# Layer 1's attention of one batch and layer 0's of the next, run as one attention of seven units

## What is computed

```python
for layer in (0, 1):
    h = layernorm(x) * (1 + ca) + sa
    x = x + ga * attention(h)        # 16 heads of 8, causal, 1024 tokens
    h = layernorm(x) * (1 + cb) + sb
    x = x + gb * experts(h)          # layer 0: 8 experts, best 2; layer 1: 16 experts, gated, best 4
# attention of layer 0: softmax(h K^T) V for all heads, then gelu, Wf, bias, residual h
# attention of layer 1: rotary q and k; 6 plain heads, 4 hyperbolic heads, 6 cosine heads
def hyp_attn(q, k, v, curv):
    inner = q k^T - sqrt(1/curv + |q|^2) * sqrt(1/curv + |k|^2)
    arg = maximum(-curv * inner, 1 + 1e-7)
    scores = 1 / (1e-6 + sqrt(1/curv) * arccosh(arg)) + causal
    return softmax(scores) v
```

## Time and profile before

| what | us |
|---|---|
| median of 3 runs (lowest, highest) | 2570.61 (2569.86, 2571.68) |
| the profiled execution | 2583.2 |
| its span, first to last instruction | 2580.8 |
| start, to the first score product of block 0 | 80.2 |
| attention of layer 0, batches 0 to 3 | 159.0, 159.8, 163.0, 161.3 |
| from there to the first score product of layer 1 (gelu, projection, layer norm, ffn(0), `prepare`), batch 1 | 118.4 |
| attention of layer 1, batches 0 to 3 | 214.7, 212.0, 211.8, 206.4 |
| output projection of layer 1, batch 1 | 8.1 |
| layer norm and ffn(1) of batch 1, with the guests of batch 2 | 127.7 |
| the same for batch 3, without guests | 112.1 |

### The profile page before, as it was taken

How to read it: one execution, slowest core, us unless ns; L and a number is a source line. 1 busy time by engine, 2 the same in 40 slices (tenths; PEclk the granted TensorE clock), 3 DMA queues, 4 the chain that set the end, 5 groups by cost and what they waited for, 6 DMA issues and landing times. The chain is left out here.

```text
span 2580.8 us, 29914 instructions
## 1 busy us (share of the span) xinstructions
PE 2141.7 (83%) x10649; PEld 851.2 (33%) x10649; DVE 1481.4 (57%) x3042; ACT 1345.0 (52%) x1923; POOL 832.4 (32%) x909
## 2 busy tenths in 40 slices
PE   6798967779999886678999987777899998677889
PEld 2232422224433342223443333222443324322243
DVE  6562557756556266675655435777665634577552
ACT  2345447973244545795224543688423454378922
POOL 1112124543411313552331221355232211145534
PEclk7899857778999896677999987667899998676789
DMA  5200231004310023100620012110051002301012
GB/s 147 66 14 12 72 99 35 2 1 123 97 28 1 18 80 85 36 1 13 157 59 20 2 50 83 48 36 1 27 153 41 20 2 83 89 10 36 1 53 87
DMA packets 67845, 128.31 MB, mean 50 GB/s; under 512 B 11396, under 2 KB 24836, under 8 KB 63076
## 3 DMA queue, kind: packets, MB, share of 16 engines
q1 hardware_dynamic: 67696, 126.40, 17.8%
HBM read 109.99 MB, written 15.20 MB: 49 GB/s over the span
## 5 line engine op out<-in xcount | busy, mean ns | idle before, releaser
L1267 DVE TENSOR_REDUCE mx<-ps 128x1 f32<-128x512 f32 (+3 forms) x992 | 612.5, 655 | 377.8 <-PE ps L607 246.9
L1015 ACT ACTIVATE pr<-ps 128x1024 f32<-128x1024 f32 (+3 forms) x672 | 515.8, 805 | 407.6 <-PE ps L677 407.0
L604 PE MATMUL ps<-kop,qop 72*128 72x512 bf16 (+6 forms) x1248 | 430.1, 378 | 110.3 <-DVE mx L1267 68.7
L677 PE MATMUL ps<-qop,kop 75*128 75x512 bf16 (+7 forms) x1344 | 412.1, 370 | 118.0 <-DVE wb L1329 41.6
L1558 POOL TENSOR_SCALAR_AFFINE_SELECT pr<-pr 128x512 f32<-128x512 f32 x224 | 144.9, 647 | 739.8 <-ACT pr L1015 739.1
L723 PE MATMUL ps<-pr,vt 128*32 128x512 f32 (+3 forms) x2688 | 339.5, 582 | 8.4 <-POOL pr L1558 7.8
L1076 ACT ACTIVATE pr<-ps 128x512 f32<-128x512 f32 x224 | 133.8, 598 | 341.9 <-PE ps L832 278.3
L604 PEld LDWEIGHTS ps<-kop,qop 72*128 72x128 bf16 (+1 forms) x1248 | 129.4, 106 | 443.5 <-DVE mx L1267 256.8
L677 PEld LDWEIGHTS ps<-qop,kop 75*128 75x128 bf16 (+1 forms) x1344 | 121.9, 105 | 357.1 <-ACT pr L1015 116.7
L842 PE MATMUL ps<-pr,w_down 128*128 128x512 f32 x384 | 196.5, 598 | 4.1 <-POOL pr L1549 4.1
L829 PE MATMUL ps<-hT,w_gate 128*128 128x512 f32 x384 | 196.2, 592 | 0.2 <-DVE on L1494 0.2
(11 more groups left out here) (313 smaller groups left out, 3089.1 us busy)
## 6 DMA issues: line engine op xcount, KB each, us to landing
wb<-gates_scratch SPq DMA_DIRECT2D x192, 256.0 KB, 3.4
kop<-kparts_scratch SPq DMA_DIRECT2D x32, 576.0 KB
qop<-qparts_scratch SPq DMA_DIRECT2D x96, 192.0 KB
on<-hmax_scratch SPq DMA_DIRECT2D x8, 1024.0 KB, 5.6
kparts_scratch<-on SPq DMA_DIRECT2D x12, 256.0 KB, 2.9
qparts_scratch<-on SPq DMA_DIRECT2D x12, 256.0 KB, 4.5
qparts_scratch<-wb SPq DMA_DIRECT2D x12, 192.0 KB
kparts_scratch<-wb SPq DMA_DIRECT2D x12, 192.0 KB
```

Source lines behind the costliest of these rows:

```text
L604: mm = pe.matmul(o, qop[0:k, slot(l, u), j, qb * P:(qb + 1) * P], kop[0:k, slot(l, u), j, k0:k0 + wd], start=True, stop=not diag)
L677: mm = pe.matmul(o, kop[0:k, slot(l, u), 2 * pair + j, kb * P:(kb + 1) * P], qop[0:k, slot(l, u), 2 * pair + j, q0:q0 + wd], start=True, s ...
L1015: nc.scalar.activation(pr[:, g % 3, 2 * pair:2 * pair + 2, o0:o0 + wd], ps[:, bank:bank + 2, o0:o0 + wd], ACT.Exp).then_inc(a.exps, 1)
L1267: ins_ = nc.vector.tensor_reduce(mx[:, nth(l, u) % 2, j0:j0 + heads, qb, col % 2], ps[:, bank, 0:heads * wd].rearrange("p (j n) -> p j n", ...
```

## The change

Block b now holds the attention of layer 1 of batch b-1 and that of layer 0 of batch b as one loop over seven units, 84 positions, in the order of `units`. The experts of layer 1 come one block later (batch b-2), and there are six blocks. Block 4 has layer 1's attention of batch 3 alone, with half-steps at positions 2 to 25; block 5 the last ffn(1).

```diff
-HYP_POS = [1 + k for k in range(HYP_HALVES)]
+def units(b):
+    if b == 0:
+        return [(0, 0), (0, 1), (0, 2), (0, 3)]
+    if b < B:
+        return [(1, 0), (0, 0), (0, 1), (1, 1), (0, 2), (0, 3), (1, 2)]
+    return [(1, 0), (1, 1), (1, 2)] if b == B else []
+def hyp_positions(b):
+    if 1 <= b < B:
+        return [3 + 3 * k if k < 8 else 32 + 3 * (k - 8) for k in range(HYP_HALVES)]
+    return [2 + k for k in range(HYP_HALVES)] if b == B else []
...
+    elif b < B:
+        hyp_pieces(0, 0, 1)
+        unit_pieces(1, 2, 8)
+        unit_pieces(2, 15, 20)
+        hyp_pieces(1, 24, 28)
+        unit_pieces(3, 28, 32)
+        for n in (4, 5, 6):
+            unit_pieces(n, NS * (n - 1) + 3, NS * (n - 1) + 8)
+        for c in range(NC):
+            plan[36 + c].append(("xT", (c,)))
```

Standard units now alternate between two of the three operand slots, the hyperbolic unit keeps the third, and each unit's operands are loaded when the unit two before it has ended. The hyperbolic values no longer accumulate in PSUM, since bank 5 holds layer 0's sums: a side job "hv" multiplies one step (two half-steps) into bank 6 or 7, and VectorE adds it to `hacc`:

```diff
+                    elif kind == "hv":
+                        i = what[0]
+                        c, kb, q0, wd, _ = STEPS[i]
+                        o0 = q0 - c * CH
+                        acc, o = hacc[:, o0:o0 + wd], ps[:, bank, o0:o0 + wd]
+                        if kb == 0:
+                            ins_ = nc.vector.tensor_copy(acc, o)
+                        else:
+                            dve.wait_ge(J.side_out, count("hv", (i - 1,)))
+                            ins_ = nc.vector.tensor_tensor(acc, o, acc, ALU.add)
```

More of the change, by code:

```diff
@@ L15 @@
 SLOTS = 3
-HYP_RING = 5
 PAIRS = 3 * HD * 3
@@ L53, with layer @@
 OPS_HYP = OPS + 16 * (1 + 2)
+HYP = 7
+def units(b):
[4 more added lines that the diff above has]
+    return [(1, 0), (1, 1), (1, 2)] if b == B else []
+UN = [units(b) for b in range(B + 2)]
+def layer(b, n):
+    return 1 if n == HYP else UN[b][n][0]
 def diagonals(g):
```

1295 lines of the change are left out of this document (666 added, 629 removed).

## The result

| what | before | after |
|---|---|---|
| median (lowest to highest) | 2570.91 (2569.86 to 2571.68) | 2810.62 (2807.57 to 2832.83) |
| the profiled execution | 2583.2 | 2832.8 |
| its span | 2580.8 | 2831.1 |
| its two attentions of a pair, or its joint attention, three of each | 374.5, 375.0, 373.1 | 456.9, 453.7, 454.9 |

The changed kernel takes 1.0951 times as long (95% interval 1.0895 to 1.1008). 2652 us were forecast; the measured median lies outside the range of 2495 to 2720 us. All rows of the changed kernel come from its one profiled execution, which was 0.8% (22 us) over its median. The window of the first joint attention starts 0.8 us ahead of its first score product, the others at theirs.

A forecast was written before the change was run, and what follows sets the result against it. Layer 0's attention was taken as TensorE's, layer 1's as ScalarE's. Other terms summed to +4.4 us, so span = 1462.6 + 3 J; J = 400 gave 2662.6, execution 2665.0, scaled to the median 2652 us, range 2495 to 2720.

The forecast's parts named there:

- J: Time of one joint attention of seven units, forecast at 400 us; the kernel gets slower if it is over 372.7 us.
- Start: First maxima's DMA waits behind late loads until 80.2 us; with 3 MB less in front, -4.5 us (0 to -7).
- Block 1's operands and the barrier: Batch 1's operands run alone, uncovered by ffn(1), +30 us (22 to 36); one more barrier, +1.5 us.
- The stretches before blocks 2, 3 and 4: Between attentions: ffn(1) -1, -1 and -15.6 us, output of layer 1 half hidden, -4 us each.
- eleven first hyperbolic groups: Batch 3's attention: formerly run during a load wait, now after the border with nothing to hide them, +7 us (0 to 10).
- Reloading 4 MB of weights in a block: DMA is little busy and no load is waited for: 0 us; without that cover 18 us a block.
- I ask of every position which engine has most in it: Joint attention priced position by position by its largest engine, since engines go in step; gave J = 400 us.
- windows with pieces: Joint attention: five wide positions with 7.2 groups each, VectorE largest at 6.8 us a position, 34 us together.
- The plain positions: Positions without pieces, one half-step in three: 14.3 us for three wide ones, against 8.2 in layer 0 without half-steps.
- the chain: A half-step's dependent steps in plain positions, little older work as filler; ScalarE idle 1 to 2 us before the root.
- B: Joint attention: loads overlap, the chain hides behind pieces and TensorE's backlog; J 345, 2488 us, chance 0.28.
- C: Joint attention: TensorE's clock falls too, through pauses at most positions; J 425, 2727 us, chance 0.07.

The follow-up runs named there:

- e11: Kernel before, with the first unit's maxima sent ahead of the late weight loads in the first batch: 2570.48 us, ratio 0.9983.
- e7: Kernel before, with the pieces of layer 0's attention at positions 3 to 8 instead of 0 to 8: 2662.47 us, ratio 1.0336.
- e5: Changed kernel without the half-steps, their value products and the hyperbolic output's turn in the three joint attentions: 2470.08 us, ratio 0.9584.
- e1: Changed kernel, with the products with ones computed for layer 1's units of the joint attention too (not used): 2831.69 us, ratio 1.1014.
- e10: e7 with up to two side jobs run between the value products and the products with ones: 2598.65 us, ratio 1.0091.
- e9: Changed kernel, with up to two side jobs between value products and products with ones in layer 0's units: 2764.63 us, ratio 1.0733.
- e4: Changed kernel, with half-steps in six groups of four neighbouring positions instead of every third position: 2872.28 us, ratio 1.1174.
- e12: Changed kernel, with half-steps two positions apart and mostly outside the positions with pieces: 2826.42 us, ratio 1.0976.
- e3: Changed kernel, with a half-step's scores right after its position's values, ahead of the remaining side jobs: 2943.36 us, ratio 1.1464.
- e13: e5 with up to two side jobs between value products and products with ones in layer 0's units: 2418.07 us, ratio 0.9407.

## Why the prediction was wrong

**The formula held; J did not.** Span = 1462.6 + 3 J gives 2828 us for the measured mean of 455.2, and 2831.1 us were measured. The sum of the small terms was forecast at +4.4 us and is +7.4 us:

- Start: -4.5 forecast, -3.5 measured (first score product at 76.7 us). e11 shows that the late loads ahead of the send are the cause: 3.2 us from the send to the product, when nothing is queued before it.
- Block 1's operands and the barrier: +31.5 forecast, +37.1 measured (157.4 against 120.3 us). The term that was short is the value projection, 14 us forecast and 22 us with its idle time in the rows below, 1140 ns a product against 720 in the earlier trace rows. The granted clock in it is 0.50, all at the lower level, where it was 0.83 in the kernel before (24 to 33 us): with one bank TensorE waits for ScalarE's copy between the products.
- The stretches before blocks 2, 3 and 4: -5, -5 and -19.6 forecast; against the same stretches of before -7.8, -6.9 and -13.3.
- Batch 3: its eleven first hyperbolic groups, +7 forecast, lie ahead of the first score product and so in the stretch before block 4. There they run from 2489.8 to 2496.8 us with nothing to hide them, 7.0 us, and with them that stretch's forecast is -19.6 + 7 = -12.6 against the -13.3 measured. The attention itself: -1.2. The end of the kernel: 0 forecast, +3.4 measured. Layer 0's attention of batch 0: -0.4.
- Reloading 4 MB of weights in a block: 0 forecast, and nothing in these sums asks for more.

The value projection of block 1, the clock there, and the first of the eleven groups and the first score product of block 4:

```profile
L593 PE MATMUL ps<-w_wv,hT 128*128 128x512 f32 x16 | 16.6, 1140 | 5.5 <-ACT vt L954 4.7 <-ACT xin L949 0.8
```

```profile
370.00:393.50 23.50, 18.00 (x18) 4.21 (x18) 4.39 (x5) 4.78 (x8) 0.00 (x0) 0.50 0.55 129
```

```profile
2489.80 0.22 PE L675 MATMUL ps<-kop,qop 84*128 84x128 bf16 x1
...
2496.81 1.91 PE L748 MATMUL ps<-qop,kop 72*128 72x512 bf16 x4
```

**The step that failed** is "I ask of every position which engine has most in it", applied to the windows with pieces. For five wide positions with 7.2 groups each it gave 5.3 us of TensorE, 4.9 of VectorE, and 6.8 with a half-step in three positions. The group's price came from whole units of the kernel before, (41.6 - 29.5)/38 = 0.32 us, a mean over nine positions with one to six groups, of which 31 of the 38 lie between score products. The change moves groups to positions that have their four slots full, and the price of the next one is 0.93 us (e7, from which this price is taken). e7's window without half-steps took 36.0 us and e5's 37.7, where the method gives 34 - 5/3 x 3.7 = 28 us for the five wide positions and the narrow one took 2.4 us in e7, 30 us together. So the window of (0,2) was priced 6 to 8 us too low. A joint attention has five such windows. In e5's second one they took 34.8, 30.6, 38.2, 37.7 and 33.3 us, 174.6 us together; against five times 30 that is some 25 of the 55 us by which J was missed. Two of them, those of (0,1) and (1,1):

```profile
1100.10:1130.70 30.60, 28.16 (x176) 8.81 (x174) 20.19 (x44) 14.55 (x23) 2.54 (x3) 0.88 0.09 35
1142.90:1181.10 38.20, 33.38 (x156) 10.86 (x156) 24.33 (x44) 11.83 (x12) 1.38 (x3) 0.73 0.01 3
```

**What a window's half-steps add** was about right: 47.0 - 37.7 = 9.3 us, and 39 - 30 = 9 us in the sum.

**The plain positions** too: 28.2 us in (0,2), and in (1,1) 77.3 - 49.1 = 28.2 again, against 29. But two links of the chain that gave them were off in opposite directions, so that this agreement is in part luck. In the second joint attention ScalarE idles before the root for 31.5 + 25.7 + 15.1 us (one group for each buffer), 3.0 us a half-step, where 1 to 2 were forecast, but before the log for only 0.5 us. In sum (0,2): +8 for the window, -1 for the plain positions: 68 forecast, 75.2 measured.

**The largest miss of one unit is (1,0)**, and no run takes it apart:

```profile
1096.50:1168.90 72.40, 59.67 (x277) 19.01 (x276) 44.86 (x79) 35.34 (x47) 15.53 (x18) 0.63 0.14 37
```

It took 72.4 us where 57 were forecast. The others took 63.2, 63.8, 77.3, 75.2, 66.9 and 34.3 us where 55, 55, 68, 68, 61 and 31 were forecast, 3 to 9 us more each. (1,0) has up to seven groups in a position, and layer 1's units have three slots between score products instead of four, so that the dearer price may hold there as well; this is argued only. As far as it is shown, the price of a group explains somewhat under half of the miss of J.

**The rivals.** The measured J of 455 us lies above that of every rival. B (the loads overlap, J 345) is refuted by it, and e5 shows by how much: even with no half-step at all, 340.7 us are used, 4 us short of B's whole time. C (J 425, chance 0.07) named the right symptom: 0.74 of mean clock against the 0.75 to 0.9 expected. As a cause it is weaker than it looks. The same instructions of unit (0,0) in the second and third joint attention, and of (0,3), show what clock and time do together:

```profile
1868.80:1928.70 59.90, 47.45 (x342) 15.81 (x341) 35.37 (x67) 34.69 (x50) 16.85 (x26) 0.93 0.09 21
1168.90:1232.10 63.20, 52.75 (x343) 17.37 (x341) 35.56 (x67) 34.81 (x50) 16.87 (x26) 0.83 0.08 20
2145.30:2219.10 73.80, 59.17 (x357) 17.46 (x349) 38.39 (x61) 40.51 (x54) 22.40 (x26) 0.74 0.07 17
1448.40:1515.30 66.90, 52.96 (x337) 15.87 (x341) 37.96 (x61) 40.47 (x54) 22.56 (x26) 0.82 0.08 19
```

0.1 of clock goes with 3.3 us in one unit and 0.08 with 6.9 us in another. A lower clock may cost this time, or longer pauses may make both. And e1 raised the clock in (1,1) by 0.18 for nothing, and e10 got it back to 1.00 by an order alone. What the clock took by itself, beside the pauses that lowered it, wasn't separated.

The Trainium skill (Perfetto Trace Analysis, Optimization Strategy) says that interleaving regimes with different busiest engines may help. Here it cost 81 us a block. The same section advises to find the gaps of the engine that one optimizes for and what ends them. e9 and e10 do that and won 46 and 64 us; but the engine whose gaps counted was VectorE, which was the busiest in neither regime's total.

**Where it came from**: two operand slots instead of three forced six positions instead of nine. The prediction saw this, and priced it at nothing beyond the count of groups.

**What stays open.** A half-step costs 4.7 us in the joint attention and 3.0 us in layer 1's alone. That is 42 us more a block, half of the loss, and its cause is open. Neither of two other places was cheaper (e4, e12). Its order behind the side jobs (e3 moved two things), its ring of four buffers instead of five, the separate accumulation and the clock weren't tried one by one. The 8 us by which e13 is over the separate attentions and the groups that moved in are not assigned either; a load of operands for which the slot has to come free first is one candidate, which is argued only.

## What to carry to other kernels

Price a moved job at the place where it goes, by the next one there, and not by its mean where it stood: here 0.30 us for groups that nearly all lay in a slot between products, 0.93 us for groups that nearly all stood behind them. Where two engines hand work to each other through two banks, "the largest engine of the position" is a lower bound; add the time in which the consumer has nothing because the producer does something else. And if a long run of the producer has the consumer idle, put two hand-overs into the middle of it before moving anything larger.

## What the runs showed of the hardware

TensorE was busy for 83% of the window of (1,1), 40.9 of 49.1 us, and its granted clock there was 0.60. Being busy by the profile's count did not keep the upper level of 2.4 GHz. In that clock TensorE's busy time is hardly a measure of work: 2392 matmuls took 370.0 us at 0.81, 2105 took 368.1 us at 0.74, 1785 took 356.8 us at 0.68.
